# Kept sums added on VectorE instead of by identity products; three expansions moved from VectorE to ScalarE

## What is computed

```
def ggc(x, adj, W, wih, whh, bih, bhh):        # gated graph convolution
    m = adj @ (x @ W)
    r, z = sigmoid(of the r and z parts of m @ wih.T + bih and x @ whh.T + bhh)
    n = tanh(i_n + r * h_n)
    return (1 - z) * n + z * x
h  = relu(ggc(x, adj, ...1))
x1 = layernorm(x + relu(ggc(h, adj, ...2)))
# layer 1: the last 100 nonzero entries of each row of adj, weighted 0.5 ** (distance from the end)
out = layernorm(x1 + w(adj != 0) @ (x1 @ weight) + bias)
```

## Time and profile before

| | |
|---|---|
| median of 3 runs | 345.53 us (345.31 to 345.88) |
| the profiled execution, its own time | 346.18 us |
| its span in the profile | 344.1 us |
| busy share of the span, TensorE / VectorE / ScalarE / GpSimd | 96% / 87% / 55% / 14% |
| granted TensorE clock, mean | 0.998 |
| second pass, from the gates of step 8 to those of step 15 | 205.15 to 304.52 us |

### The profile page before, as it was taken

One profiled execution on the slowest core, in us unless ns is written; L12 is line 12 of the kernel. 1 busy time (PEld: TensorE's weight loads), 2 busy tenths in 40 slices (PEclk: granted clock), 3 DMA queues, 4 the chain that ended last, 5 costly groups with the idle time before them and its releaser, 6 DMA issues.

```text
span 344.1 us, 6780 instructions
## 1 busy us (share of the span) xinstructions
PE 328.7 (96%) x2540; PEld 154.0 (45%) x2540; DVE 299.2 (87%) x494; ACT 187.6 (55%) x245; POOL 47.2 (14%) x50
## 2 busy tenths in 40 slices
PE   1998999999999999999999999999999999999993
PEld 0442334333333333333333333546364544789993
DVE  0689879899999999997999678878999999968996
ACT  0203304105122047068467437897977869768995
POOL 2000000000000000000000001250514232233275
PEclk9999999999999999999999999999999999999999
DMA  6999999999999998999898999998999996000003
GB/s 240 414 410 409 410 407 410 404 402 367 399 396 370 366 392 327 351 360 352 291 336 301 378 368 381 392 344 324 339 379 391 346 381 249 4 16 4 2 2 123
DMA packets 32143, 107.85 MB, mean 313 GB/s; under 512 B 3568, under 2 KB 6512, under 8 KB 32112
## 3 DMA queue, kind: packets, MB, share of 16 engines
q1 hardware_dynamic: 31248, 106.15, 81.4%
q10 hardware_dynamic: 864, 1.28, 1.1%
HBM read 106.37 MB, written 1.05 MB: 312 GB/s over the span
## 4 chain that ended last, share of the span: by engine, by line
PE 78%; DMA 10%; DVE 8%; issue 2%; POOL 0%; ACT 0%; POOLq 0%; ACTq 0%; DVEq 0%; SPq 0%
PE m_acc L509 41%; PE out L509 17%; DMA stream<-in_adj_t 9%; PE out L647 8%; PE gate_ps L585 4%; DVE codes L1241 3%; PE gate_ps L592 3%; PE m_acc L647 2%; DMA w<-in_w 2%; PE gate_ps L609 1%; PE gate_ps L614 1%; DVE s_in L1298 1%; DVE codes L1052 1%; DVE stream L1305 1%; PE m_acc L556 1%
## 5 line engine op out<-in xcount | busy, mean ns | idle before, releaser
L509 PE MATMUL m_acc<-stream,s_in 128*64 128x512 f32 x488 | 119.1, 596 | 1.2 <-DMA stream<-in_adj_t 0.9
L1052 DVE TENSOR_SCALAR codes<-stream 128x1024 uint8<-128x1024 f32 x109 | 71.8, 686 | 6.4 <-DMA stream<-in_adj_t 6.2
L509 PE MATMUL out<-stream,s_mid 128*64 128x512 f32 x264 | 66.3, 593 | 0.0
L968 POOL TENSOR_TENSOR rstd<-stat,mhalf 128x4 f32<-128x4 f32 (+1 forms) x17 | 25.6, 1510 | 277.2 <-DVE stat L1207 277.1
L509 PEld LDWEIGHTS m_acc<-stream,s_in 128*64 128x64 f32 x488 | 32.8, 136 | 63.7 <-issue 48.4
L509 PE MATMUL m_acc<-stream,s_mid 128*64 128x512 f32 x224 | 51.8, 600 | 0.2 <-DMA stream<-in_adj_t 0.2
L1101 DVE SCALAR_TENSOR_TENSOR codes<-codes,run 128x384 uint32<-128x384 uint32 (+2 forms) x62 | 45.4, 732 | 2.1
L1096 DVE TENSOR_TENSOR run<-run,codes 128x768 uint16<-128x768 uint16 (+2 forms) x61 | 43.6, 715 | 2.0
L745 ACT ACTIVATE m_high<-m_acc 64x512 f32<-64x512 f32 x13 | 7.7, 594 | 56.3 <-PE m_acc L509 47.7
L842 ACT ACTIVATE wexp<-codes,code_bias 128x2048 uint16<-128x2048 uint8 x18 | 35.7, 1992 | 0.1
L509 PEld LDWEIGHTS out<-stream,s_mid 128*64 128x64 f32 x264 | 18.9, 137 | 37.1 <-issue 36.4
(11 more groups left out here) (179 smaller groups left out, 413.4 us busy)
## 6 DMA issues: line engine op xcount, KB each, us to landing
stream<-in_adj_t SPq DMA_DIRECT2D x192, 512.0 KB, 6.1
wexp<-in_adj_t SPq DMA_DIRECT2D x2, 512.0 KB, 5.5
late<-in_adj_t SPq DMA_DIRECT2D x2, 512.0 KB, 6.6
third<-in_x_pairs SPq DMA_DIRECT2D x8, 128.0 KB, 6.2
out_nodes<-stream SPq DMA_DIRECT2D x7, 128.0 KB, 2.0
hx<-in_x_pairs ACTq DMA_DIRECT2D x1, 512.0 KB, 7.1
third<-in_adj_t SPq DMA_DIRECT2D x1, 512.0 KB, 8.0
run<-in_adj_t SPq DMA_DIRECT2D x1, 512.0 KB, 9.5
```

The source lines that it names most:

```text
L509: last = nc.tensor.matmul(to[D * u:D * (u + 1), :], state[:, t * D:(t + 1) * D], data[:, u * CW:(u + 1) * CW], start=start[u], stop=stop)
L968: nc.gpsimd.tensor_tensor(rstd[:, r, nodes], stat[:, r, nodes], mhalf[:, nodes], ALU.pow).then_inc(rstd_made, 1)
L1052: nc.vector.tensor_scalar(edges(p // 2, b, 2 * (p % 2), 2), loaded(n), 0.0, None, ALU.not_equal).then_inc(mask_made, 1)
```

## The change

- The products with `ident2` go. In their place `high_kept` on VectorE forms `m_high` = accumulator half + kept sum for steps 11 to 15, between `residual` and `combine`. `high` on ScalarE goes for these five steps.
- Blocks (1, 5), (2, 5) and (3, 5) are expanded by ScalarE instead of VectorE: in stages 4 and 5 one expansion more stands before `split_high`, and in stage 7 one more before it. VectorE has none in stages 4 and 5, and two in place of three in stage 6.
- Chain tile (4, 3) goes from stage 3 to stage 2 on VectorE.
- Block (4, 1) takes place "h", and place "k" is held until `high_kept(14)` has read it.

```
+WITH_KEPT = range(NCH + 3, 2 * NCH)
...
+PLACE[4, 1] = "h"
...
-BY_DVE = [AHEAD[4], AHEAD[6], AHEAD[7], AHEAD[8]] + \
+BY_DVE = [AHEAD[7]] + \
...
-    [(4, 3), REST[0], REST[1]] + \
-    [block for block in REST[2:] if block not in BY_DVE]
-ACT_EXPANDS = {1: (0, 2, 1), 2: (1, 2, 2), 3: (1, 3, 2), 4: (1, 2, 2), 5: (1, 2, 2),
-               6: (1, 2, 2), 7: (0, 1, 1), 8: (0, 2, 4)}
-DVE_EXPANDS = {1: (0, 0, 0), 2: (0, 0, 0), 3: (0, 0, 0), 4: (0, 0, 1), 5: (0, 0, 1), 6: (0, 0, 3),
+    [(4, 3), REST[0], REST[1], (5, 3), (6, 0), AHEAD[8]] + \
+    [block for block in REST[2:] if block not in BY_DVE + [(5, 3), (6, 0)]]
+ACT_EXPANDS = {1: (0, 2, 1), 2: (1, 2, 2), 3: (1, 3, 2), 4: (1, 3, 2), 5: (1, 3, 2),
+               6: (1, 2, 2), 7: (0, 2, 1), 8: (0, 2, 4)}
+DVE_EXPANDS = {1: (0, 0, 0), 2: (0, 0, 0), 3: (0, 0, 0), 4: (0, 0, 0), 5: (0, 0, 0), 6: (0, 0, 2),
                7: (1, 0, 1), 8: (1, 1, 5)}
...
-PLACE_USED.update({"m": len(LOADS), "x": NCH * NP, "k": USED[2 * NCH - 3] + 2})
+PLACE_USED.update({"m": len(LOADS), "x": NCH * NP})
...
-CHAIN = [chain_tiles(*x) for x in ((0, 6), (6, 12), (12, 16), (16, 21), (21, 25), (25, 29), (29, 32),
+CHAIN = [chain_tiles(*x) for x in ((0, 6), (6, 12), (12, 17), (17, 21), (21, 25), (25, 29), (29, 32),
...
                 pair(n, q, s_mid, acc_bank(g), [first] * 2, n == USED[g] - 1).then_inc(pair_used, 1)
-                if first and ch in KEPT:
-                    half, _, part = kept_part(ch)
-                    pe.wait_ge(m2_kept, len(KEPT))
-                    for u in range(2):
-                        nodes = slice(u * HW, (u + 1) * HW)
-                        nc.tensor.matmul(acc_bank(g)[u * D:(u + 1) * D, nodes], ident2[half, :],
-                                         part[:, nodes], start=False, stop=False)
...
                 if t < NCH:
-                    high(g + 1)
+                    if g + 1 not in WITH_KEPT:
+                        high(g + 1)
...
+            def high_kept(g):
+                _, _, part = kept_part(2 * NCH - 1 - g)
+                dve.wait_ge(pair_used, USED[g])
+                dve.wait_ge(m2_kept, len(KEPT))
+                dve.wait_ge(m_ready, g)
+                nc.vector.tensor_tensor(m_high[0:D, :], acc_bank(g)[D:P, :], part, ALU.add)\
+                    .then_inc(high_copied, 1)
...
                 residual(g)
+                if g + 1 in WITH_KEPT:
+                    high_kept(g + 1)
                 if t < NCH:
                     combine(g + 1)
```

More of the change, by code:

```diff
@@ L841, in expand @@
                     act.wait_ge(h_made, NCH + 4)
+                if PLACE[j, i] == "k":
+                    act.wait_ge(high_copied, 2 * NCH - 1)
                 nc.scalar.activation(weights(j, i).bitcast(U16), block(j, i), ACT.Relu,
@@ L1240, in expand @@
                     dve.wait_ge(h_made, NCH + 4)
+                if PLACE[j, i] == "k":
+                    dve.wait_ge(high_copied, 2 * NCH - 1)
                 nc.vector.tensor_scalar(weights(j, i).bitcast(U16), block(j, i), float(P),
```

## The result

The changed kernel takes 347.25 us in the median of 7 runs (346.66 to 348.58), the kernel before 345.53 (345.31 to 345.88, 7 runs): a ratio of 1.0047, 95% interval 1.003 to 1.0064. A second set gave 347.07 against 345.64, ratio 1.0035 (1.002 to 1.005). It is slower by some 1.4 to 1.7 us. The profiled execution took 346.93 us, with a span of 345.0; the one of before took 346.18, with 344.1.

What follows compares the result with a forecast made beforehand. TensorE was taken as the bound, VectorE and ScalarE close behind; its 2.92 us gain eaten up and 0.26 more lost gave 346.18 + 0.26 = 346.44 profiled, 345.8 at the median. Range 343.5 to 346.8, likeliest case 345.0 to 346.4.

Steps and rivals of the forecast that it cites:

- the price of the addition: What each of five additions adds to VectorE's list: 0.684 us plus some 0.04 for combine's wait, taken as 0.72.
- VectorE becomes the bound, slower: Rival, chance 0.24: VectorE's round makes stage 6 late, stage 7's extra expansion is paid in full, 0.93 us lost, 346.5.
- The walk: Stage-by-stage pass through the lists of TensorE, ScalarE and VectorE; its outcome, 0.26 us lost, had chance 0.46.
- S(11): Start of ScalarE's sigmoids for step 11, put at 250.6 us.
- N(12): Start of VectorE's first n_input instruction for step 12, put at 266.6 us by VectorE's round.
- node(12): TensorE's node products of step 12 in stage 4, put at 269.69 us, a gain of 1.14.
- TensorE's 2.92 us: Whole possible gain: four kept sums' identity products in stages 2 to 5, 0.73 us each, if TensorE stays the bound.
- X of stage 3: Start of split_high on ScalarE in stage 3, put at 246.5 us, behind make_x1s.
- N(10): VectorE's first n_input of step 10, behind the moved tile: 234.0 us, with 0.37 lost beside GpSimd's addition.
- The shift carried to the median: The 0.26 us loss, worked out on one profiled execution, applied to the median of 345.53 to give 345.8.
- The first gives nothing: Dropping the first kept sum's products gains nothing, as they stand ahead of a transfer wait that ended at 214.53.
- ScalarE catches up: Rival, chance 0.22: costs on ScalarE and VectorE hidden up to stage 6, stage 7 still binds, gain 2.0 us, 343.5.

Runs made afterwards that it cites:

- c1: Kernel before with VectorE adding the kept sums of steps 12 and 13 alone, blocks (1, 5), (2, 5) on ScalarE: 344.53 us against 345.64, ratio 0.9966.
- a1: Kernel before with the five additions alone, expansions and tile left where they were: 3.26 us slower than before.
- g1: Kernel after with high_kept waiting for m2_kept at step 11 alone; the addition stayed in place relative to its neighbours, whole time not given.
- f2: c1 with block (3, 5) moved to ScalarE in stage 7: ratio 0.9991 to before; 1.09 us behind c1 from gates(10) to the sigmoids of stage 8.
- g2: As g1, also without the addition's wait for m_ready: 77.08 us from gates(10) to the sigmoids of stage 8, 0.44 shorter than the kernel after.
- b1: Kernel after with block (3, 5) back on VectorE in stage 6: 0.73 us slower than the kernel after by the medians.
- b2: Kernel after with chain tile (4, 3) back in stage 3: 0.59 us faster than the kernel after by the medians.
- f1: Kernel after with step 11's identity products back and its addition taken off VectorE in stage 3: 345.77 us against 345.38 for before.

## Why the prediction was wrong

The forecast was 345.8 with no change the likeliest, and a range up to 346.8; measured was 347.25, slower. The step that failed first is the price of the addition, 0.72 us where the runs showed 0.90. The mechanism was right: what came is the rival "VectorE becomes the bound, slower", to which the prediction gave 0.24. The walk names the engine that is late in each stage, and the marks in the kernel after lie close to it up to stage 6: S(11) 250.42 (walk 250.6), N(12) 266.57 (266.6), node(12) 269.51 (269.69), N(13) 282.23 (282.06), node(13) 285.13 (285.0). TensorE's 2.92 us were eaten up where it said.

The sizes were off. Of the 1.46 us between forecast and result, 0.49 is the shift between the two profiled executions (0.75 us measured, 0.26 forecast), and 0.97 comes from carrying it to the medians. In the order of the walk:

- **The price of the addition.** "I take 0.72; the bounds are 0.60 and 0.80." It is 0.90, outside the bounds. The rows gave the duration rightly (0.684 forecast, 0.69 measured), but the sum counted only how late `combine` starts behind the addition. It left out that the addition itself starts 0.46 us behind the residual's start where `combine` had started 0.34 behind. In the kernel after this counts four times, as the prediction says of it: in X of stage 3, in N(12), in N(13) and in X of stage 6, 0.7 us in all. About half of that was given back by N(10), which came 0.38 us earlier than in the walk, so the early marks lie so close to it in part by luck.
- **The standstill of stage 6**, in no row of before: L1117 starts 1.13 us behind the addition where it starts 0.78 behind in the other stages, 0.35 lost. With the addition's surplus it puts X of stage 6 at 292.68 (walk 292.0), S(14) at 296.78 (296.1), node(14) at 300.18 (299.53) and S(15) at 307.35 (306.6). That the slow rival's marks are met within 0.05 us (N(14) 297.27 for its 297.26, node(15) 310.75 for its 310.74) is luck in part too: 0.35 of the way is this standstill, which it had not reckoned with, and its sum of 346.5 was still 0.75 too low.
- **The shift carried to the median.** "The same shift on the median gives 345.8." The walk had measured against one execution of before that stood 0.65 us above its kernel's median; the profiled execution of the kernel after stood 0.32 below its own (346.93 against 347.25). Of the 0.65, the second profile of before puts 0.25 into stages 1 and 2 (25.93 against 25.68 from gates(8) to gates(10)) and 0.32 in front of gates(8) (205.15 against 204.83). In the kernel after N(10) doesn't hang on gates(10) at all but on the tile, so an execution in which before runs well in these stages shows a larger loss. What differs in front of gates(8) is not explained.

Point by point, the rest. The products: 0.73 us in stage 2, as forecast. "The first gives nothing" held, but by another wait than the one named. c1 has the products of step 11 and a1 has not, and gates(10) come 24.77 and 24.73 us behind gates(8). TensorE's timeline of a1:

```profile
214.11 1.06 PE L580 MATMUL gate_ps<-mx,third 128*64 128x256 f32 x8
...
216.31 1.96 PE L642 MATMUL out<-late,wexp 128*128 128x128 f16 x32 [0.54 <-POOL late L980]
```

and of c1:

```profile
215.24 1.03 PE L587 MATMUL gate_ps<-mx,third 128*64 128x256 f32 x8
...
216.80 1.96 PE L649 MATMUL out<-late,wexp 128*128 128x128 f16 x32
```

Without the products gates(9) follow gates(8) after 9.32 us (204.79 to 214.11) in place of 10.00 (205.24 to 215.24), so no transfer held them in a1; but then the first share waits 0.54 us for GpSimd's `split_low`, and the 0.68 are gone. In other executions a transfer does come last in stage 1, by 0.18 us in the kernel after and by 1.29 in g1.

The tile: N(10) came at 233.62, just outside the walk's bounds of 233.7 and 234.4, because the instruction ahead of the tile started 0.45 us earlier than before (228.13 against 228.58). GpSimd's addition beside it:

```profile
228.59 2.77 POOL L975 TENSOR_TENSOR s_in<-late,third 128x256 f32<-128x256 f32 x1
```

The tile's first instruction takes 1.63 us in place of 1.21, a loss of 0.42, more than the 0.37 taken. It starts at 230.81, 0.03 us behind its predecessor's end, with 0.55 us of the addition left. By the rule of the Trainium skill, page SBUF — State Buffer, section "Who interferes with whom", it would have waited for all of that. N(10) would then have been near 233.75, an estimate from these rows; the trace shows 0.13 us less. It can't be told from one row whether the instruction was blocked for a part or slowed over its length. The prediction's row for the loss was read too kindly: in stage 3 of before not one but two instructions were stretched beside such an addition, L1101 at 246.20 (1.58 us) and L1096 at 247.88 (1.57).

The third expansion of stage 7: paid as in the slow rival, 1.09 us by f2. A slip in the walk's stage 5 had no effect: its first sum for X gives 276.5, not 277.0 (266.6 + 8.48 + 0.72 + 0.71), and the second, 276.97, is the one that binds.

A wait that the walk missed: `gates(g)` also waits for `make_x1s` (L578 of the kernel before), seen as 0.79 us at 246.42; it decided nothing, since ScalarE was later still.

Of the signs to look for, ScalarE had no idle time ahead of the sigmoids of stages 4 to 7, and TensorE had gaps ahead of L604, though of other sizes than said: 0.24 us in stage 4 (with 0.79 ahead of its gates), none in stage 5, 0.74 in stage 6, 1.05 in stage 7, and in stage 8 0.34 instead of more. The slow sign "N(11) past 252" did not show: N(11) was at 250.91, and the slow case came by stage 6, not by stage 3. The rival "ScalarE catches up" fell in every run with five additions. c1, with two, comes nearest to it: TensorE's windows are full up to stage 6.

## What to carry to other kernels

When work leaves the bounding engine for one that is busy nine tenths of the time, walk the lists: which instruction waits last in each stage, and what is queued behind it. Move only as many pieces as the receiver has room for, stage by stage; here two of five gained 1.1 us, and all five, with the moves made for them, lost 1.4 to 1.7. Price an inserted instruction by the distance between the starts of its neighbours with and without it, not by its duration, and measure a shift against more than one execution before carrying it to a median.

## What the runs showed of the hardware that was not expected

- An addition of 0.69 us put between two instructions of VectorE, the second of which now waits for its result, moves the second by 0.90 us, and dropping two of its fulfilled waits changes neither distance (g1, g2). In c1 both distances stand in one kernel: 0.35 us from the residual to `combine` in stage 3 (234.64 to 234.99), 0.46 from the residual to the addition in stage 4 (251.98 to 252.44).
- VectorE stood still for 0.44 to 0.46 us ahead of one `combine` with no releaser in the profile, at the same instruction in all five profiles of four kernels (after, twice, b1, b2, g1). It is absent in g2, a1 and f1, which have the same two instructions there. The two executions of the kernel after both have it, so it goes with the program and not with the execution. Its cause is open.
- A chain tile behind the 2.65 us instruction lost 0.42 us on its first instruction while GpSimd's addition ran; that addition lasted 2.77 us in both kernels.
